# Phase 0 of a cross-attention and MoE kernel: V's context products by halves of the contraction, two tiles of x normalized on ScalarE, one low part of V on VectorE

## The reference, cut to what matters

```
def _layernorm(x, eps=1e-5):  m, v = mean(x), var(x);  return (x - m) / sqrt(v + eps)

z = _layernorm(x)                                # x: (4, 512, 1024)
hidden = concatenate([ctx_4096, z], axis=1)      # ctx_4096: (4, 64, 1024)
q = z @ Wq.T                                     # 16 heads of 96
k = hidden @ Wk.T ; v = hidden @ Wv.T            # 4 kv heads of 96
x = x + (softmax(q k^T / sqrt(96)) v) @ Wo.T
n = _layernorm(x)
x = x + layernorm_affine(relu(n @ up_w)**2 @ down_w
                         + sum(top2(n @ gate_w)) * ((n @ fc1_w) @ expert_w) @ fc2_w)
```

## Time and profile before

| what | value |
|---|---|
| median of 3 runs | 2167.39 us (2166.41 to 2169.49) |
| the profiled execution | 2169.33 us, of which the span is 2167.5 us |
| TensorE busy | 2138.7 us, 99% of the span |
| VectorE / ScalarE / GpSimd busy | 770.9 / 656.9 / 694.7 us |
| first matmul of phase 0, first of phase a | 6.30 us, 40.02 us |
| mean granted TensorE clock | 0.998 |

### The profile page before, as it was taken

One profiled execution on the slowest core, in us unless ns is written; L12 is line 12 of the kernel. 1 busy time (PEld: TensorE's weight loads), 2 busy tenths in 40 slices (PEclk: granted clock), 3 DMA queues, 4 the chain that ended last, 5 costly groups with the idle time before them and its releaser, 6 DMA issues.

```text
span 2167.5 us, 30223 instructions
## 1 busy us (share of the span) xinstructions
PE 2138.7 (99%) x9884; PEld 1762.9 (81%) x9884; DVE 770.9 (36%) x1343; ACT 656.9 (30%) x1125; POOL 694.7 (32%) x556
## 2 busy tenths in 40 slices
PE   7999999999999999999999999999999999999998
PEld 6888888887787787778888878788887888888886
DVE  4222222167777777750100213222211142222222
ACT  4111111146666666661111223212123321111111
POOL 3500000136766666672212434000004422222221
PEclk9999999999999999999999999999999999999999
DMA  5732322525555555534433535312213632222222
GB/s 174 229 136 106 126 87 88 167 86 138 138 145 148 136 145 149 123 105 144 147 115 106 198 102 174 113 63 102 72 58 132 198 101 86 85 86 87 85 88 73
DMA packets 232526, 262.42 MB, mean 121 GB/s; under 512 B 78081, under 2 KB 145921, under 8 KB 232321
## 3 DMA queue, kind: packets, MB, share of 16 engines
q1 hardware_dynamic: 184464, 182.60, 26.9%
q10 hardware_dynamic: 47984, 78.85, 12.8%
HBM read 168.46 MB, written 92.67 MB: 120 GB/s over the span
## 4 chain that ended last, share of the span: by engine, by line
PE 95%; DMA 2%; DVE 1%; issue 1%; POOL 1%; ACT 0%; SPq 0%; DVEq 0%; ACTq 0%; POOLq 0%
PE psum L116 30%; PE psum L117 29%; PE psum L118 29%; PE psum L841 3%; PE psum L210 1%; PE psum L887 1%; PE psum L888 1%; DMA operands<-operands 0%; DMA recip_scratch<-small 0%; PE psum L1473 0%; PE psum L1472 0%; PE psum L848 0%; DVE staging L198 0%; DMA staging<-in_x 0%; DMA operands<-recip_scratch 0%
## 5 line engine op out<-in xcount | busy, mean ns | idle before, releaser
L116 PE MATMUL psum<-operands 128*128 128x512 f32 (+3 forms) x2952 | 1147.8, 389 | 12.9 <-DVE operands L325 8.1
L117 PE MATMUL psum<-operands 128*128 128x512 f32 (+3 forms) x2952 | 1136.1, 385 | 0.0
L118 PE MATMUL psum<-operands 128*128 128x512 f32 (+3 forms) x2952 | 1133.9, 384 | 0.0
L116 PEld LDWEIGHTS psum<-operands 128*128 128x128 f32 (+1 forms) x2952 | 555.8, 188 | 121.3 <-DVE operands L325 9.3
L118 PEld LDWEIGHTS psum<-operands 128*128 128x128 f32 (+1 forms) x2952 | 556.1, 188 | 108.9
L117 PEld LDWEIGHTS psum<-operands 128*128 128x128 f32 (+1 forms) x2952 | 557.2, 189 | 96.0
L772 POOL TENSOR_TENSOR operands<-staging,operands 128x512 fp32r<-128x512 f32 x192 | 247.8, 1294 | 165.9 <-ACT operands L932 165.8
L996 DVE TENSOR_REDUCE small<-psum 128x1 f32<-128x576 f32 x256 | 193.4, 755 | 140.4 <-PE psum L841 140.4
L1101 POOL TENSOR_TENSOR operands<-staging,operands 128x512 fp32r<-128x512 f32 x92 | 118.4, 1297 | 367.0 <-ACT operands L1096 366.9
L1700 POOL TENSOR_TENSOR operands<-operands 128x640 fp32r<-128x640 f32 x64 | 100.3, 1570 | 319.5 <-ACT operands L1695 319.3
L1552 DVE TENSOR_TENSOR staging<-staging 128x512 f32<-128x512 f32 x64 | 45.3, 726 | 303.7 <-ACT staging L1518 302.9
(11 more groups left out here) (95 smaller groups left out, 1127.5 us busy)
## 6 DMA issues: line engine op xcount, KB each, us to landing
h_scratch<-staging ACTq DMA_DIRECT2D x80, 256.0 KB, 2.1
operands<-h_scratch SPq DMA_DIRECT2D x64, 320.0 KB, 3.1
operands<-recip_scratch SPq DMA_DIRECT2D x64, 192.0 KB, 3.1
o_scratch<-staging SPq DMA_DIRECT2D x64, 192.0 KB, 3.5
operands<-o_scratch SPq DMA_DIRECT2D x64, 192.0 KB, 2.7
operands<-q_hi_scratch ACTq DMA_DIRECT2D x14, 768.0 KB, 6.2
operands<-q_lo_scratch ACTq DMA_DIRECT2D x14, 768.0 KB, 6.7
staging<-in_x SPq DMA_DIRECT2D x20, 512.0 KB, 3.8
```

The costliest lines, as they stand in the source:

```text
L116: e.matmul(o, lh, rh, start=first, stop=False)
L117: e.matmul(o, lh, rl, start=False, stop=False)
L118: return e.matmul(o, ll, rh, start=False, stop=last)
```

## The change

Four edits, all in phase 0; batches 1 to 3 and the other phases keep their instructions.

1. **V's products by halves.** Both products run k = 0 to 3 first (they need lows 10, 11, 12), then both run k = 4 to 7. The transposes move with the second half: step 0, 1, 2 ahead of (0, 4) as before, steps 6 and 7 ahead of (1, 4) and (1, 5). The wait for the last lows of GpSimd now stands ahead of the first transpose.
2. **Two tiles on ScalarE.** VectorE normalizes tiles 0 and 2. Tiles 1 and 3 are done in place by ScalarE in two passes: subtract the mean (Identity with bias `nmean`, a new 4-column instruction on VectorE) and multiply by `rstd` (Copy with scale). The centering stands between the square root and high 13, the scaling behind high 15.
3. **A dummy square root** behind high 4, which loads the root's table there.
4. **Low 12 on VectorE**, behind the reciprocal and ahead of the copy of the root; GpSimd keeps 10, 11, 13, 14, 15.

```
-        BY_DVE, BY_POOL = list(range(10)), list(range(10, NF))
+        BY_DVE, BY_POOL = [*range(10), 12], [10, 11, 13, 14, 15]
 # dve_norm
+                if by_tile:
+                    e.tensor_scalar(nmean, mv[:, :, 0], -1.0, None, ALU.mult).then_inc(cp, 1)
                 link(e.tensor_scalar(ve, mv[:, :, 1], EPS, None, ALU.add))
                 link(e.reciprocal(rec, ve))
+                if by_tile:
+                    by_tile(ST)
 ...
-                for t in range(ST):
+                for t in (0, 2) if by_tile else range(ST):
                     z = e.tensor_scalar(xn[:, t, :], xn[:, t, :], mv[:, t, 0:1], rstd[:, t:t + 1], ALU.subtract, ALU.mult)
 ...
+            def act_center(e, t):
+                e.wait_ge(*past(cp, 1))
+                e.activation(xn[:, t, :], xn[:, t, :], ACT.Identity, bias=nmean[:, t:t + 1]).then_inc(cx, 1)
+            def act_scale(e, t):
+                e.wait_ge(*past(ch, LN_CHAIN))
+                e.wait_ge(*past(cx, (t + 1) // 2))
+                e.activation(xn[:, t, :], xn[:, t, :], ACT.Copy, scale=rstd[:, t:t + 1]).then_inc(zn, 1)
 # p0_pe
-            at = {(0, 4): [0, 1, 2], (0, 5): [3], (0, 6): [4], (0, 7): [5], (1, 0): [6], (1, 1): [7]}
-            for t in range(2):
-                for k in range(DK):
+            at = {(0, 4): [0, 1, 2], (0, 5): [3], (0, 6): [4], (0, 7): [5], (1, 4): [6], (1, 5): [7]}
+            e.wait_ge(*past(w_lop, 2))
+            e.wait_ge(*past(w_lod, len(BY_DVE)))
+            for hf in range(2):
+                if hf:
+                    e.wait_ge(*past(w_lop, len(BY_POOL)))
+                for t in range(2):
+                    for k in range(hf * DK // 2, (hf + 1) * DK // 2):
 ...
 # p0_act
-            for n in range(13):
+            for n in range(5):
+                raw_high(e, n)
+            e.wait_ge(*past(ph_start, 2))
+            e.activation(sm[:, 336:337], ident[:, 0:1], ACT.Sqrt)
+            for n in range(5, 13):
                 raw_high(e, n)
             a_sqrt(e, 0, rt_ps)
+            for t in (1, 3):
+                a_center(e, t)
             for n in range(13, NF):
                 raw_high(e, n)
+            for t in (1, 3):
+                a_scale_z(e, t)
 # p0_dve
-            a_norm(e, 0, lambda t: raw_low(e, 6 + t, w_lod))
+            a_norm(e, 0, lambda t: raw_low(e, BY_DVE[6 + t], w_lod))
```

More of the change, by code:

```diff
@@ L127, in xattn_ffn_kernel @@
         rt_ps, nt_ps = PS[:, 7, 0:ST], PS[:, 7, 8:8 + ST]
+        nmean = sm[:, 340:344]
         def norm_z(tag, xn, last_free, first=(6, 7), tiles=False):
@@ L141, in norm_z @@
             sq = sem(f"{tag}_sqrt")
-            cp = sem(f"{tag}_sqrt_copied")
+            cp, cx = sem(f"{tag}_copied"), sem(f"{tag}_centered")
+            own = 2 if tiles else 0
             zn = sem(f"{tag}_z")
@@ L188, in dve_norm @@
                     e.tensor_copy(rt, rt_ps).then_inc(cp, 1)
-                    e.wait_ge(*past(cp, 1))
+                    e.wait_ge(*past(cp, 2))
                     e.sem_inc(idle, 1)
@@ L206, in pe_t @@
                 if k == 0:
-                    e.wait_ge(*past(zn, b + 1))
+                    e.wait_ge(*past(zn, b + 1 + own))
                 e.wait_ge(*past(zl, b * DK + k + 1 - len(banks(b))))
@@ L223, in dve_lo @@
                 e.tensor_tensor(zlo[:, k, :], z_bank(b, k), raw(zhi[:, k, :]), ALU.subtract).then_inc(zl, 1)
-            return load, load_tile, dve_norm, act_sqrt, pe_t, act_hi, dve_lo, zl, fr, zt
+            return load, load_tile, dve_norm, act_center, act_scale, act_sqrt, pe_t, act_hi, dve_lo, zl, fr, zt
         def mm_groups(e, b, groups, lo_sem, wait_bank, slot_of, done, slot_ready=None, after_group=None, free=None, pe_t=None):
@@ L382, in p0_pe @@
             e.wait_ge(*past(ph_start, 2))
-            at = {(0, 4): [0, 1, 2], (0, 5): [3], (0, 6): [4], (0, 7): [5], (1, 0): [6], (1, 1): [7]}
-            for t in range(2):
-                for k in range(DK):
[L386 to L392, removed]
+            at = {(0, 4): [0, 1, 2], (0, 5): [3], (0, 6): [4], (0, 7): [5], (1, 4): [6], (1, 5): [7]}
[6 more added lines that the diff above has]
+                    for k in range(hf * DK // 2, (hf + 1) * DK // 2):
+                        for q in at.get((t, k), []):
+                            a_pet(e, 0, q)
+                        ch, cl = (z[:, k * BC + t * P:k * BC + (t + 1) * P] for z in cT)
+                        m = parts3(e, c_bank(KC + t), ch, cl, v_w[0][:, k], v_w[1][:, k], k == 0, k == DK - 1)
+                        if k == DK - 1:
+                            m.then_inc(c_mm, 1)
         def p0_act(e):
@@ L443, in xattn_ffn_kernel @@
         A_EV = NQK + ST
-        a_load, a_load_tile, a_norm, a_sqrt, a_pet, a_hi, a_lo, a_zl, a_fr, a_zt = norm_z(
+        a_load, a_load_tile, a_norm, a_center, a_scale_z, a_sqrt, a_pet, a_hi, a_lo, a_zl, a_fr, a_zt = norm_z(
             "a", XN, lambda e, b: e.wait_ge(*past(a_acc, b * A_EV)), (5, 6, 7), True)
@@ L1150, in xattn_ffn_kernel @@
         d_acc = sem("d_product", 20)
-        d_load, _, d_norm, d_sqrt, d_pet0, d_hi, d_lo, d_zl, d_fr, d_zt = norm_z(
+        d_load, _, d_norm, _, _, d_sqrt, d_pet0, d_hi, d_lo, d_zl, d_fr, d_zt = norm_z(
             "d", XN2, lambda e, b: e.wait_ge(*past(d_acc, b * ND)))
```

## The result

| | before | changed |
|---|---|---|
| median, 20 runs each | 2168.43 us (2166.41 to 2169.61) | 2163.65 us (2162.26 to 2165.72) |
| ratio | | 0.998, 95% interval 0.9973 to 0.9986 |
| profiled execution (its span) | 2169.33 (2167.5) | 2165.72 (2163.9) |

The change made the kernel faster, by 4.8 us between the medians and by 3.0 to 5.9 us by the interval; 2.2 us had been forecast. The changed kernel's profiled execution is the slowest of its 20 runs, 2.1 us above their median, and that of before is 0.9 above its own.

A forecast was written before the change was run, and what follows sets the result against it. TensorE was taken as the bound, behind a 40.02 us start. First transpose at 29.35 plus 8.45 us put phase a at 37.8, 2.2 us less: 2165.2 us on the median, range 2162.2 to 2168.3.

The forecast's parts named there:

- The mechanism: TensorE, phase 0: 12 matmuls move ahead of the transposes, taking 2.08 us from the part before the first 128x512 matmul.
- the clock stays up: TensorE behind the first transpose: after a 2.35 us gap the granted clock stays at 1.0, 1.8 us less.
- The dummy: ScalarE behind high 4: early table load costs 0 to 0.25 us, taken as 0; saves 1.28 us at 20.15.
- The small instructions: VectorE: `nmean` ends at 20.20, low 11 then goes ahead of epsilon; 1.27 us delay, early table's gain lost.
- Low 12: VectorE ahead of the root's copy: starts at 21.9, takes 0.69 us, ends at 22.6; normalization at 24.2 against 23.34.
- Two tiles on ScalarE: ScalarE: passes of 1.03 us hold high 13 to 24.1; GpSimd ends last, first transpose at 29.35, 0.8 us later.
- Transposes to phase a: TensorE from first transpose to first 128x512 matmul: 8.45 us with the clock up, 9.37 if it falls.
- The hold-up of step 6: TensorE's transposes: step 6 waits for VectorE's low part 3 of z, 5.5 us against 4.6, giving 0.9 us back.
- the clock falls all the same: Rival, TensorE behind the 2.35 us gap: clock falls, phase a at 38.7, gain 1.3 us, 2166.1 us; chance 22%.
- epsilon isn't held up: Rival, VectorE: reciprocal ends at 20.65, phase a at 37.2, gain 2.8 us, 2164.6 us; chance 25%.
- slower: Rival, GpSimd's last low ends at 30.95, clock falls, phase a at 40.4, 0.4 us later, 2167.8 us; chance 7%.
- better: Rival: lows and tiles overlap, step 6 isn't held up; phase a at 35.5, gain 4.5 us, 2162.9 us; chance 8%.

The follow-up runs named there:

- the repetitions of before: The unchanged kernel profiled three times more: 2167.7, 2167.22 and 2168.17 us.
- nine traces: Traces of the kernels with V's products by halves, the changed kernel and its variants; medians 2163.6 to 2165.07 us.
- D: Not a run: the first small instruction behind the statistics, an event read in every trace; 19.52 us before, 20.71 us in the changed kernel.
- the halves alone: The kernel before with only V's products by halves, the transposes with the second half: 2164.40 us, ratio 0.9984.

## Why the prediction was right, and short by half

*The mechanism.* The point of measurement (the first 128x512 matmul) and V's halves taking 2.08 us from behind the transposes were right. That the clock stays up came true, but I had argued it from a gap of 2.35 us being nearer to 2.01 than to 3.46; the gap was 1.70, and as the repetitions of before show, its length doesn't settle it, so this term was in part luck. 10.06 and 10.10 of before against 7.97 to 8.03 in nine traces give 2.1 us for the moved matmuls; the fall of the clock adds 1.4 where it happens.

*The dummy.* Right: table load at 7.90, high 5 at 9.31 instead of 9.17, nothing behind it, no drain. The Trainium skill's drain (ScalarE: Activation LUTs, "What ACT_TABLE_LOAD costs") doesn't show in these traces either: from 7.90 to the activation at 9.20 is the load alone.

*The small instructions.* `nmean` took 0.68 us, as foretold. "So I take it that low 11 goes first" was wrong: epsilon followed in 0.16 us, and low 11 started at 21.32, with epsilon already in. In all seven traces that have the pair it took 0.15 or 0.16 us. The row at 24.36 that I took as nearest was one long instruction behind another with a low already asking; two short ones in a row got through. That was the wrong step in phase 0: the root came 1.11 us behind D, not 2.4.

*Low 12.* It was forecast as free at 0.69 us; since low 11 was now still running, it took 1.22, and the copy of the root stood behind it. The early root (0.8 us) was lost there: the copy came 2.36 us behind D and had come 2.25 before. The rule of the Trainium skill (SBUF — State Buffer, "Who interferes with whom") is that a VectorE instruction with two inputs in SBUF contends with a GpSimd instruction that reads SBUF. The trace agrees: 1.22 us against 0.69. No case of mine had this term.

*Two tiles on ScalarE.* Passes of 1.13 us, 1.04 apart (1.03 forecast); high 13 held up to 24.01; low 15 last. All as foretold, but 1.1 to 1.3 us earlier against D (high 13 at 3.30 us behind it, 4.58 forecast), and with GpSimd idle for 2.10 us and not 3.3. I had put the first transpose 29.35 - 19.52 = 9.83 us behind D; it was 8.71, and 9.05 before. So edits 2 to 4 gave 0.3 us where I had them cost 0.8. That is 1.1 us of the shortfall.

*Transposes to phase a.* 8.45 forecast, 7.99 measured. The hold-up of step 6, 0.9 us of the sum, did not happen:

```profile
33.54 0.68 DVE L240 TENSOR_TENSOR operands<-psum,operands 128x512 fp32r<-128x512 f32 x1
34.27 0.34 PE L118 MATMUL psum<-operands 128*128 128x384 f32 x1
34.44 0.60 PE L227 MATMUL psum<-ident,staging 128*128 128x128 f32 x4
```

Low part 3 of z was done at 34.22, 4.80 us behind the first transpose (5.5 forecast), and TensorE came to step 6 at 34.44 without a wait. Lows follow each other at 0.6 us (the first of VectorE's line 240 at 30.74, the third at 31.95), not at the 0.86 that I took from waits of before. The one wait of TensorE for line 240 stood ahead of step 3, at 31.49, about 0.2 us; with slightly slower steps it makes 0.4 instead of the 0.9. That is 0.5 us.

*The sum.* Against before's traces with a fall: 0.34 + 2.08 + 1.38 = 3.8 us at the same D; without a fall, 2.4. The mean over the four traces of before is 3.1. Of the 4.8 us between the medians, 1.7 stay unassigned; 0.8 may be the stretch behind phase 0, and the interval of the ratio (3.0 to 5.9) reaches down to 3.1. That part was not settled. The rivals: "the clock falls all the same" did not happen on the path in any trace; "epsilon isn't held up" is what happened, with 2.8 us the nearest case by its mechanism; "slower" did not happen; the "better" case (4.5 us, 2162.9) is nearest by size, and one of its two conditions held, the step 6 that isn't held up. The lower end of the range, 2162.2, doesn't follow from its working: 2164.6 less 1.0 is 2163.6. The 2163.65 lies just inside that too. Phase a at 37.41 and 36.70 lies between the 36.5 and 39.5 that I had set.

## What to carry to other kernels

Where one engine bounds a kernel but for its start, look for work of that engine that doesn't need the late input and move it ahead of the wait: here 12 matmuls were worth more than three edits that made the input earlier. Before giving an instruction from GpSimd to VectorE or ScalarE, check in whose queue it then stands ahead of the critical one: low 12 stood ahead of the copy and took back the early root, and centering stood ahead of high 13 and left GpSimd idle for 2.1 us. And read such a start from an event behind the loads: their chance (1.5 us here) is larger than what three of the four edits gave (0.3 us).

## What the runs showed that I had not expected

The granted clock falls behind gaps of about 2 us in some executions and not in others of the same kernel: ahead of V's products the gap is 2.01 us in the first trace of before, and the clock stayed up; it is 2.00 to 2.01 us in the three repetitions, and it fell to 1.2 GHz for 3.4 us each time. Whether a fall costs anything is decided by what stands under it: 1.4 us under transposes that phase a waits for, 0 to 0.1 us under V's products ahead of them (9.05 and 9.06 us from D to the first transpose in the repetitions of before, 9.10 with the halves alone).
